# Diagonal score blocks of a causal attention kernel: four column tiles of unequal length, four signals for one, and a new table of places

## The reference

```python
q = _apply_rope(split_heads(x @ W_q)); k = _apply_rope(split_heads(x @ W_k)); v = split_heads(x @ W_v)
scores = jnp.einsum('bhqd,bhkd->bhqk', q, k)
scores = jnp.where(jnp.triu(ones((s, s)), k=1), -jnp.inf, scores)      # key after query: left out
attn = jax.nn.softmax(scores / jnp.sqrt(jnp.float32(hd)), axis=-1)
ctx = jnp.einsum('bhqk,bhkd->bhqd', attn, v)
```

## Time and profile before

| | |
|---|---|
| median of 3 runs | 2454.95 us |
| profiled execution | 2453.28 us |
| its span, first to last instruction | 2451.5 us |
| granted TensorE clock, mean share | 0.977 |
| busy: PE, DVE, ACT, POOL | 93%, 82%, 73%, 43% |

### The profile page before, as it was taken

How to read it: one execution, slowest core, us unless ns; L and a number is a source line. 1 busy time by engine, 2 the same in 40 slices (tenths; PEclk the granted TensorE clock), 3 DMA queues, 4 the chain that set the end, 5 groups by cost and what they waited for, 6 DMA issues and landing times. The chain is left out here.

```text
span 2451.5 us, 96050 instructions
## 1 busy us (share of the span) xinstructions
PE 2291.6 (93%) x38509; PEld 1359.8 (55%) x38509; DVE 2011.2 (82%) x5739; ACT 1789.7 (73%) x4319; POOL 1049.5 (43%) x1252
## 2 busy tenths in 40 slices
PE   7979994999999999999999999999999999899787
PEld 6767771544554445554444545444454454688676
DVE  7979988898998988999988989989889996354444
ACT  6767771888888888888887888888888888555111
POOL 6979995222233333333333333333233333222666
PEclk9989995999999999999999999999999999999999
DMA  6898987677765565665655655656656551797998
GB/s 214 288 273 286 294 271 162 159 164 165 165 117 100 112 117 93 117 113 106 114 103 137 115 107 109 120 98 113 114 100 110 112 103 29 235 318 262 308 334 269
DMA packets 302572, 406.28 MB, mean 166 GB/s; under 512 B 99248, under 2 KB 233648, under 8 KB 302000
## 3 DMA queue, kind: packets, MB, share of 16 engines
q1 hardware_dynamic: 289840, 366.58, 60.7%
q0 software_dynamic: 12288, 33.57, 5.6%
HBM read 225.46 MB, written 173.02 MB: 163 GB/s over the span
## 5 line engine op out<-in xcount | busy, mean ns | idle before, releaser
L970 DVE CUSTOM_DVE_ANT_0 dump<-ps_rows,mask 128x128 bf16<-128x128 f32 (+7 forms) x2048 | 1471.3, 753 | 164.7 <-issue 139.5
L940 ACT ACTIVATE probs<-ps_cols 128x512 f32<-128x512 f32 (+3 forms) x3072 | 1316.8, 499 | 272.8 <-PE ps_cols L1112 256.0
L1112 PE MATMUL ps_cols<-q_st,k_st 99*32 99x512 bf16 (+3 forms) x12288 | 877.5, 328 | 12.4 <-issue 7.0
L1046 PE MATMUL ps_rows<-k_st,q_st 96*32 96x128 bf16 (+3 forms) x12288 | 828.4, 331 | 26.0 <-issue 9.2
L906 POOL TENSOR_SCALAR_AFFINE_SELECT probs<-probs 128x512 f32<-128x512 f32 x512 | 325.0, 635 | 1064.2 <-ACT probs L940 1060.2
L1088 PE MATMUL ps_ctx<-probs,v_st 128*32 128x512 f32 (+3 forms) x6144 | 639.2, 487 | 6.0 <-issue 4.8
L1112 PEld LDWEIGHTS ps_cols<-q_st,k_st 99*32 99x32 bf16 x12288 | 328.8, 95 | 349.0 <-ACT probs L940 171.7
L1046 PEld LDWEIGHTS ps_rows<-k_st,q_st 96*32 96x32 bf16 x12288 | 296.0, 96 | 387.5 <-DVE row_max L970 233.6
L1088 PEld LDWEIGHTS ps_ctx<-probs,v_st 128*32 128x32 f32 x6144 | 173.4, 110 | 98.2 <-POOL probs L906 15.5
L970 DVE DVE_READ_ACCUMULATOR2_ANT row_max<- 128x1 f32 x2048 | 171.1, 84 | 0.0
L1382 PE MATMUL ps_t<-w_o_sb,cT 128*128 128x256 f32 x512 | 127.8, 407 | 30.5 <-DVE prod L1323 30.5
(11 more groups left out here) (115 smaller groups left out, 2563.5 us busy)
## 6 DMA issues: line engine op xcount, KB each, us to landing
parts_dram<-parts SPq DMA_DIRECT2D x64, 768.0 KB, 4.1
q_st<-parts_dram SPq DMA_DIRECT2D x384, 128.0 KB
k_st<-parts_dram SPq DMA_DIRECT2D x384, 128.0 KB
xs_dram<-zeros SPq DMA_DIRECT2D x36, 512.0 KB, 6.7
xs_sb<-xs_dram SPq DMA_DIRECT2D x72, 256.0 KB, 4.8
g_dram<-g_sb SPq DMA_DIRECT2D x72, 256.0 KB, 3.6
v_dram<-v_sb SPq DMA_DIRECT2D x32, 544.0 KB, 5.0
v_st<-v_dram SPq DMA_DIRECT2D x64, 272.0 KB
```

Of the source, the lines that this page charges most:

```text
L940: nc.scalar.activation(probs[:, k % PB, h, 0:w], ps_cols[(GH * k + h) % CB][:, 0:w], ACT.Exp).then_inc(exp_done, 1)
L970: nc.vector.tensor_tensor_reduce(out=dump[:, done % 2, 0:n], in0=ps_rows[:, 512 * bank:512 * bank + n], in1=mask[:, S - n:S], scale=1.0, s ...
L1046: mm = nc.tensor.matmul(ps_rows[a:a + VW, 512 * (bank + c):512 * (bank + c) + w], q_st[r][0:KS, i // IB, q0 + a:q0 + a + VW], k_st[r][0:KS ...
L1112: mm = nc.tensor.matmul(ps_cols[(GH * k + h) % CB][a:a + VW, 0:w], k_st[r][:, j // IB, k0 + a:k0 + a + VW], q_st[r][:, c, h * 512 + q0 - 5 ...
```

## The change

The matmuls of a block that meets the diagonal stop at it, tile by tile. In a row block, the tile that holds queries a to a+31 needs no key beyond a+31 of the last 128, so it is 96 - a columns shorter. In a diagonal column block, the tile with keys a to a+31 needs no query before a, so it starts a columns later. The rest of the bank keeps what was there; the mask and the zeroing cover it. In the rows ahead of the first group and the first column step of all, everything is computed in full.

Since tiles of unequal length can end in another order than they are issued, each tile signals, and a slot or column block is ready at four increments (two by two for the two tiles of the transposed maxima). Two semaphores are used in turn, by the parity of the slot or block, so that increments of a following block are not taken for those that are missing. `pv_done` too is now raised by all four tiles of the values, and its thresholds are multiplied by four.

`ITEMS` and `ORDER`, the table of places, are new. The number of R, V, M and X in them is the same. Of the diff of the two tables some lines are shown:

```diff
-    slot_ready = sem("slot_ready")
+    slot_ready = [sem(f"slot_ready{u}") for u in range(2)]
-    cols_ready = sem("cols_ready")
+    cols_ready = [sem(f"cols_ready{u}") for u in range(2)]
...
-    ITEMS = [(0, 2), (1, 0), (1, 1), (0, 3), (1, 2), (2, 0), (3, 2), (3, 0),
+    ITEMS = [(1, 3), (1, 1), (2, 1), (1, 2), (2, 3), (3, 3), (3, 2), (3, 0),
...
-        ("R", "RR", "RR", "VR"),
-        ("", "RRM", "RV", "R"),
+        ("RR", "", "R", "VRR"),
+        ("RR", "M", "R", "V"),
...
+    TILES = P // VW
+    def wait_slot(eng, slot):
+        eng.wait_ge(slot_ready[slot % 2], TILES * (slot // 2 + 1))
+    def wait_cols(eng, i):
+        eng.wait_ge(cols_ready[i % 2], TILES * (i // 2 + 1))
...
-                    sp.wait_ge(pv_done, NS * n)
+                    sp.wait_ge(pv_done, GH * NS * n)
...
-        def row_item(r, t, slot, bank, before):
+        def row_item(r, t, slot, bank, before, stairs=True):
...
-                w = min(512, n - 512 * c)
+                last = n <= 512 * (c + 1)
                 for a in range(0, P, VW):
+                    w = n - 512 * c - (P - VW - a if stairs else 0) if last else 512
...
-            mm.then_inc(slot_ready, 1)
+                    if last:
+                        mm.then_inc(slot_ready[slot % 2], 1)
...
                     for a in range(0, P, VW):
-                        mm = nc.tensor.matmul(ps_cols[(GH * k + h) % CB][a:a + VW, 0:w],
+                        o = a if diag and (n > 0 or k > 0) else 0
+                        mm = nc.tensor.matmul(ps_cols[(GH * k + h) % CB][a:a + VW, o:w],
                                               k_st[r][:, j // IB, k0 + a:k0 + a + VW],
-                                              q_st[r][:, c, h * 512 + q0 - 512 * c:(h + 1) * 512],
+                                              q_st[r][:, c, h * 512 + q0 - 512 * c + o:(h + 1) * 512],
                                               start=True, stop=True, tile_position=(0, a))
-                    mm.then_inc(cols_ready, 1)
+                        mm.then_inc(cols_ready[at % 2], 1)
```

More of the change, by code:

```diff
@@ L693, in attention_phase @@
     ORDER = (
-        ("R", "RR", "RR", "VR"),
-        ("", "RRM", "RV", "R"),
[L696 to L700, removed]
+        ("RR", "", "R", "VRR"),
+        ("RR", "M", "R", "V"),
+        ("R", "R", "XR", "R"),
+        ("R", "VRR", "", ""),
+        ("RVR", "", "R", "V"),
+        ("R", "", "RV", "R"),
+        ("", "R", "", "R"),
+        ("", "R", "V", "R"),
+        ("", "XM", "", "RV"),
         ("R", "", "R", "V"),
[L702 to L705, removed]
+        ("R", "", "R", "V"),
+        ("RV", "R", "", "V"),
     )
@@ L916, in move_max @@
         def move_max(n, c, slot, bank):
-            act.wait_ge(slot_ready, slot + 1)
+            wait_slot(act, slot)
             if n > 0:
@@ L930, in copy_ctx @@
         def copy_ctx(n, c):
-            act.wait_ge(pv_done, NS * n + HALF_END[c])
+            act.wait_ge(pv_done, GH * (NS * n + HALF_END[c]))
             nc.scalar.activation(ctx_raw[:, c, :], ps_ctx[:], ACT.Copy).then_inc(ctx_copied, 1)
@@ L936, in group @@
                 if not (first and k < PB):
-                    act.wait_ge(pv_done, NS * n + k - PB + 1)
+                    act.wait_ge(pv_done, GH * (NS * n + k - PB + 1))
                 for h in range(GH):
-                    act.wait_ge(cols_ready, GH * (NS * n + k) + h + 1)
+                    wait_cols(act, GH * (NS * n + k) + h)
                     nc.scalar.activation(probs[:, k % PB, h, 0:w], ps_cols[(GH * k + h) % CB][:, 0:w],
@@ L966, in row_item @@
                 dve.wait_ge(rows_done, done - 1)
-            dve.wait_ge(slot_ready, slot + 1)
+            wait_slot(dve, slot)
             dve.nop(nofuse=True)
@@ L1058, in transpose_max @@
                 b = min(a + VW, PARTS * GH * IB)
-                mm = nc.tensor.transpose(small_bank(bank)[a:b, 0:P], parts[:, a:b], ident_b[:], tile_position=(0, a))
-            mm.then_inc(slot_ready, 1)
+                nc.tensor.transpose(small_bank(bank)[a:b, 0:P], parts[:, a:b], ident_b[:], tile_position=(0, a))\
+                    .then_inc(slot_ready[slot % 2], TILES // 2)
         def transpose_ctx(n, c, slot, bank, before):
@@ L1072, in transpose_ctx @@
                                           tile_position=(0, a))
-            mm.then_inc(slot_ready, 1)
+                    if i == IB - 1:
+                        mm.then_inc(slot_ready[slot % 2], 1)
         def values(n, r, k):
@@ L1090, in values @@
                                       tile_position=(0, VW * h))
-            mm.then_inc(pv_done, 1)
+                mm.then_inc(pv_done, 1)
         pe.wait_ge(operands_loaded[0], LOAD)
         for t in range(NI):
-            row_item(0, t, *FIRST_ROWS["row", t])
+            row_item(0, t, *FIRST_ROWS["row", t], stairs=False)
         transpose_max(0, 0, *FIRST_ROWS["max", 0])
@@ L1110, in group @@
                     k0 = h * 512 + (j % IB) * P
+                    at = GH * (NS * n + k) + h
                     for a in range(0, P, VW):
-                        mm = nc.tensor.matmul(ps_cols[(GH * k + h) % CB][a:a + VW, 0:w],
+                        o = a if diag and (n > 0 or k > 0) else 0
+                        mm = nc.tensor.matmul(ps_cols[(GH * k + h) % CB][a:a + VW, o:w],
                                               k_st[r][:, j // IB, k0 + a:k0 + a + VW],
-                                              q_st[r][:, c, h * 512 + q0 - 512 * c:(h + 1) * 512],
+                                              q_st[r][:, c, h * 512 + q0 - 512 * c + o:(h + 1) * 512],
                                               start=True, stop=True, tile_position=(0, a))
-                    mm.then_inc(cols_ready, 1)
+                        mm.then_inc(cols_ready[at % 2], 1)
                     for what, arg in [e[2] for e in EVENTS if e[:2] == (k, h) and happens(e[2], n)]:
```

## The result

| | before | changed |
|---|---|---|
| first comparison, median | 2455.18 us (4 runs) | 2481.62 us (4 runs), 1.0112 of before (1.0091 to 1.0133) |
| second comparison, same chip side by side | 2449.33 us (17 runs) | 2474.40 us (6 runs), 1.0087 (1.0057 to 1.0117) |
| profiled execution, its span | 2451.5 us | 2484.6 us |
| mean distance of group starts | 25.96 us | 26.53 us |
| undisturbed distance | 25.29 us | 25.43 us |

A forecast was written before the change was run, and what follows sets the result against it. PE's array was taken as the bound. Shorter tiles less signals and new DVE waits, 1.09 - 0.25 = 0.84 us over 63 periods, saved 53 us; with 1 us for the last group, 2402 us was forecast, range 2368 to 2446.

The forecast's parts named there:

- The bound: In an undisturbed group, PE's array is the limit: 24.1 of 25.29 us filled, 1.2 us for gaps.
- The shorter tiles: Diagonal row and column blocks: fewer columns on PE save 1.09 us a group, between 0.88 and 1.29.
- the 0.60 us from steps 0 to 3: Row items among diagonal column blocks in a group's first four steps: a saving of 0.60 us, expected in any case.
- Four signals: At hand-overs from PE where somebody waits: 0.02 to 0.03 us each, 0.25 us a group with new DVE waits.
- my 15 hand-overs: In a group, up to 15 hand-overs where ACT or DVE waits; at 0.11 us each, 1.65 us.
- The table: New order of row and column items: nothing by itself, from -0.3 to +0.3 us a group.
- The stops: Irregular stops of PE between groups: 0.67 us a group, 42 us in all, expected to stay.
- D: Rival, 0.12: the signals' tail, 0.11 us on 15 waits, outweighs the shorter tiles; slower, 2478 to 2490 us.
- B: Rival, 0.15: DVE takes over and stops make tiles level; only steps 0 to 3 gain, 2431 or 2442 us.
- B's signs: In the group: DVE idle under 0.5 us, or PE standing before row blocks longer than 3.2 us.
- the one for "wrong altogether": Sign that the whole argument fails: the undisturbed period stays and the irregular stops change instead.

The follow-up runs named there:

- e8: The kernel before with every diagonal block 48 columns shorter in all four tiles, one signal, old tables: 0.9915 of before, undisturbed distance 24.86 us.
- e3: The changed kernel with the old tables (stepped tiles, four signals): 1.0154 of before.
- e2: The kernel before with four signals for one and two semaphores in turn, full tiles, old tables: 1.0208 of before.
- e14: The kernel before with the new tables alone, on another chip than e1: 1.0081 of before, undisturbed distance 25.42 us.
- e7: The changed kernel with two signals a block for four and the transposed maxima doubled onto the third and fourth tile: 1.0004 of before, undisturbed 24.95 us.
- e4: The changed kernel with full tiles (new tables, four signals): 1.0165 of before.
- e1: The kernel before with the new tables alone (full tiles, one signal): 1.0037 of before.
- e13: e7 with the old tables (shorter tiles, two signals, level transposes): 0.9963 of before, undisturbed distance 25.11 us.
- e15: e10 with ACT's exponential also leaving out the 48 uncomputed columns: 0.9766 of before.
- e11: The kernel before with four signals for row blocks and transposes alone, full tiles, old tables: 1.0086 of before.
- e12: The kernel before with four signals for column blocks alone, full tiles, old tables: 1.0067 of before.
- e10: e8 with DVE's maximum also 64 columns shorter in row items of over 128 keys: 0.9862 of before.

## Why the prediction was wrong

**The bound.** This is the step on which the gain rested, and it failed. "The PE array is the bound, with 1.2 us for gaps": the array was full, but that did not make it the bound. The sum of 24.1 us of columns in 25.29 stands; its reading was the error, since DVE, with 23.39 us of work and four banks between it and PE, was as near. With the same columns taken out evenly and nothing added, e8 got 0.43 us of 1.29. The check was in the rows: PE waited 11 times for DVE and 9 for ACT in that group. I set these aside as hidden by weight loads, and e8 shows that they grow when columns go.

**The shorter tiles, 1.09 us (0.88 to 1.29).** They gave 0.25 us with the old tables (e3 against e2) and 0.2 to 0.3 with the new (changed against e4). That the array lets tiles drift was right. What failed is that I counted columns as time: the 0.60 us from steps 0 to 3 that were to "come in any case" supposed a stretch bound by the array. In the kernel before, DVE has no wait over 0.1 us there until the end of step 3. With the new tables, these four steps take 7.17 us in an undisturbed group of e14 (full tiles, one signal), 7.10 in one of e7 (stepped, two signals) and 7.41 in one of the changed kernel.

**Four signals, 0.02 to 0.03 us a hand-over.** 0.08 us measured, and 0.6 to 0.85 us a group where I had 0.25 (e2); with the new table, 0.52 (e4 against e1). I took the low end of 0 to 0.11 because unequal tiles end apart, and they did not hide it. The 79 ns worked out from the Trainium skill stood in the text and were right; my 15 hand-overs were too many for that price (0.62 to 0.85 over 0.08 is 8 to 11).

**The table, nothing.** By itself it costs 0.13 us of the undisturbed distance and 0.4 to 0.8% in all; with four signals beside it, it gives 0.4% back (e2 to e4), and with stepped tiles too 0.4 to 0.7% (e3 to changed, on different chips). So its sign depends on what stands beside it. The most it cost, 0.3 us a group, is the edge of what I allowed. Put together: the signals alone cost 2.1%, the shorter tiles take 0.5% off, and the new table beside both takes off what is left to the 0.9 to 1.1% measured.

**The stops.** I let them stay at 42 us. They went to 55 (0.88) and 69 us (1.10) in the two executions. I had put this term at no change without a reason, and it is more than half of the loss: 0.14 x 63 = 9 us are in the undisturbed distance, while the medians are 25 to 26 us apart. Its cause stays open. Kernels with the new tables have 0.81 (e14) to 1.10 us of stops a group, before and e13 with the old ones 0.63 to 0.68; but e8 and e15, with the old tables and shorter groups, have 0.80 and 0.87.

**The rival.** D, with 0.12, had the right mechanism (the tail at hand-overs of PE with DVE and with ACT, and e11 and e12 show both rings), and the right side; its price of 0.11 us on 15 waits was too high. It supposed the tiles at their full worth, so its time (2478 and up) is met by two errors that offset each other. B, DVE taking over, has half a case: in e8 PE waits longer for DVE once columns are gone (4.1 us), but in the changed kernel's undisturbed group B's signs are missing (DVE idle for 1.8 us, PE waiting for it 9 times, 2.4 us), and e10 shows that DVE alone doesn't hold the rest. Of my signs, the one for "wrong altogether" came nearest: the undisturbed period stayed within 0.14 us, and the irregular stops grew.

A slip without weight: 2401 and 1.7 make 2403, not 2402.

## What to carry to other kernels

An engine that is full to 95% is only the bound if its neighbours have room too: where three engines stand at 85 to 95% with rings of two to four slots between them, ask by a run with the work cut evenly what the work is worth, before paying anything for taking it out. A signal more on the way from TensorE cost 26 ns here (0.08 us for three) where somebody waited, so let only those tiles signal of which one ends last. And a new order of work should be judged by the whole time, not by its undisturbed period: e7 has the shorter undisturbed period than e13 and is the slower kernel.

## What the runs showed of the hardware

- Matmuls on different column tiles of 32 start out of program order when one tile is free and another isn't (864.69 before 864.70 above).
- Three more signals of a block delay the engine that waits by 0.08 us, for ACT and DVE alike (e2 against before).
- PE stops for over 1.4 us, up to 2.5 us where the profile shows nothing that holds it, each time within about a microsecond of the start of a 16 KB instruction packet (before and changed). At some of these stops the clock falls to 1.2 GHz, and in the second execution of the changed kernel, with stops up to 2.8 us, it does not; six groups with such a fall took over 29 us.
- Chips differ: on two of those used, the shortest groups with indirect DMAs in them are 1.3 to 1.9 us longer than the shortest without, and the kernel before takes 2570 us instead of 2450. That the DMAs are the cause was not tested.
